# Expert groups of one mixture layer: 68 groups of two batches become 60 whole groups and eight half groups in float32, and their results go through DRAM instead of into sums by batch

## The reference, cut to what matters

```python
rw = softmax(router_logits); w, sel = top_k(rw, 2)          # per batch
def mlp(x, g, u, d):  return (gelu(x @ g) * (x @ u)) @ d     # 256 -> 1024 -> 256
out = sum over the two chosen experts e:  w[e] * mlp(x, gate[e], up[e], down[e])
out = out + mlp(x, shared_gate, shared_up, shared_down)
x = x + out                                                  # then layers 1, 2 and 3
```

## Time and profile before

| | |
|---|---|
| time, median of 3 runs | 1223.13 us (1220.38 to 1224.0) |
| the profiled execution | 1221.87 us, its span 1220.3 us |
| PE busy | 1195.6 us, 98% of the span |
| DVE / ACT / POOL busy | 719.9 / 466.1 / 469.6 us |
| chain that ended last | PE 91%, DVE 4%, the rest under 2% each |
| DMA | 135.31 MB, mean 111 GB/s |

### The profile page before, as it was taken

How to read it: one execution, slowest core, us unless ns; L and a number is a source line. 1 busy time by engine, 2 the same in 40 slices (tenths; PEclk the granted TensorE clock), 3 DMA queues, 4 the chain that set the end, 5 groups by cost and what they waited for, 6 DMA issues and landing times.

```text
span 1220.3 us, 26642 instructions
## 1 busy us (share of the span) xinstructions
PE 1195.6 (98%) x7370; PEld 1043.2 (85%) x7371; DVE 719.9 (59%) x1282; ACT 466.1 (38%) x877; POOL 469.6 (38%) x297
## 2 busy tenths in 40 slices
PE   8898999999999999999999999999999999899998
PEld 7798998888888888888888888889999998778876
DVE  5789686556557557566565656555555556444443
ACT  4256532322222222223223223233443333466664
POOL 2076689406336036081444563010000002875840
PEclk9899999999999999999999999999999999999999
DMA  7159772202213013021131321033344336476654
GB/s 221 44 189 312 258 265 83 83 15 65 66 32 99 15 32 99 15 86 45 47 86 45 86 67 30 17 109 103 106 110 107 98 87 236 144 238 214 205 154 121
DMA packets 133169, 135.31 MB, mean 111 GB/s; under 512 B 64640, under 2 KB 114048, under 8 KB 131072
## 3 DMA queue, kind: packets, MB, share of 16 engines
q1 hardware_dynamic: 119440, 84.87, 23.3%
q0 software_dynamic: 13680, 49.81, 13.1%
HBM read 109.48 MB, written 25.17 MB: 110 GB/s over the span
## 4 chain that ended last, share of the span: by engine, by line
PE 91%; DVE 4%; POOL 1%; issue 1%; ACT 1%; DMA 1%; SPq 0%; DVEq 0%; ACTq 0%; POOLq 0%
PE bank L630 15%; PE bank L632 15%; PE bank L631 15%; PE bank L686 10%; PE bank L1015 6%; PE bank L667 5%; PE bank L685 4%; PE bank L1044 3%; PE bank L858 2%; PE bank L737 2%; PE bank L993 2%; PE bank L739 2%; PE bank L738 2%; PE bank L688 1%; PE bank L1024 1%
## 5 line engine op out<-in xcount | busy, mean ns | idle before, releaser
L474 POOL TENSOR_TENSOR W<-raw,one 128x1024 fp32r<-128x1024 f32 x79 | 150.3, 1902 | 577.3 <-PE bank L686 349.5
L1631 DVE TENSOR_TENSOR FS<-bank,FS 128x512 f32<-128x512 f32 x200 | 138.1, 691 | 193.1 <-PE bank L632 162.8
L1102 ACT ACTIVATE FS<-bank 128x512 f32<-128x512 f32 x200 | 119.5, 597 | 322.8 <-PE bank L632 322.5
L630 PE MATMUL bank<-W,RS 128*128 (+1 forms) x576 | 225.7, 392 | 2.3 <-DVE W L1726 2.0
L632 PE MATMUL bank<-W,RS 128*128 (+1 forms) x576 | 224.9, 390 | 0.0
L631 PE MATMUL bank<-W,RS 128*128 (+1 forms) x576 | 224.8, 390 | 0.0
L686 PE MATMUL bank<-W,RS 128*128 x544 | 216.2, 419 | 0.0
L476 POOL TENSOR_TENSOR W<-raw,W 128x1024 fp32r<-128x1024 f32 x79 | 191.8, 2428 | 6.2
L1699 DVE SCALAR_TENSOR_TENSOR acc<-bank,weight,acc 64x256 f32 x272 | 131.4, 483 | 73.7 <-issue 36.9
L1109 ACT ACTIVATE RS<-bank 128x512 fp32r<-128x512 f32 x144 | 86.4, 600 | 176.2 <-PE bank L667 176.2
L630 PE MATMUL bank<-RS,W 128*128 128x256 f32 x448 | 129.9, 290 | 0.0
(11 more groups left out here) (221 smaller groups left out, 2075.2 us busy)
## 6 DMA issues: line engine op xcount, KB each, us to landing
raw<-in_w POOLq DMA_DIRECT2D x87, 512.0 KB, 4.2
mixes<-acc SPq DMA_DIRECT2D x16, 1024.0 KB, 5.6
W<-mixes SPq DMA_DIRECT2D x16, 1024.0 KB, 6.2
FS<-in_xT SPq DMA_DIRECT2D x200, 64.0 KB, 2.5
acc<-in_w SPq DMA_DIRECT2D x22, 512.0 KB, 4.2
acc<-in_b SPq DMA_DIRECT2D x8, 640.0 KB, 11.0
acc<-in_x SPq DMA_DIRECT2D x32, 128.0 KB, 3.8
raw<-in_mask POOLq DMA_DIRECT2D x8, 512.0 KB, 4.6
```

What stands on the lines that cost most here:

```text
L474: pool.tensor_tensor(hi, raw[:, k, :], ones_like(PIECE), ALU.mult).then_inc(done, 1)
L630: pe.matmul(ps, ah, bh, start=(i == 0), stop=False)
L1102: act.activation(gl[h], gate_ps[h][:, :], ACT.Gelu_apprx_tanh).then_inc(gelu_done, 1)
L1631: TT(hid[h], up_ps[h][:, :], gl[h], ALU.mult).then_inc(hid_done, 1)
```

## The change: what it does

1. Chosen groups. There are again 68 positions, but 60 of them are whole groups (128 tokens, one expert, `floor(count / 2)` for each expert) and four times two are half groups: the up to eight batches that are left over go in twos, whatever their experts, through half of the hidden units in one position (`HALVES`, positions 4 and 12 of a loop body of 16) and through the other half in another. Half groups multiply in plain float32 (`up_gate_mixed`, `down_mixed`), with weights that SP loads unsplit into `acc` rows (`load_mixed0`, six pieces for each half group).
2. Results. A whole group's result is added up in SBUF by two instructions (L1879, L1883 of the changed kernel), and `store_chosen` writes it to `chosen_rows` in DRAM by slot. In the late stage `load_chosen` brings the eight halves (64 x 256) for each unit back by eight DMAs, and `join` adds them; `cross_over` on ACT is gone, as is POOL's clearing of `acc` (`zeros_made`).
3. Routing. The tables have other contents, and their computation is cut into more and shorter portions: some after groups 2 and 3, then portions in pairs 0 to 4. `tables_ready` is now incremented in the fifth pair (index 4), and the sums on PE (`route_sums_`) stand within pair 0.
4. POOL frees a weight slot by `add_step` in place of `down_done`, and begins with layer 3's first expert after the last join (`x1_done`, NU) in place of shortly before the last down products.
5. In the last units DVE does `x2_lo` before `keep`.

The core of the diff:

```diff
-NR0 = (2 * NB + E) // 2
+NMIXED0 = E // 2
+FULL0 = NB - NMIXED0
+NR0 = FULL0 + 2 * NMIXED0
+HALVES = (4, 12)
@@ PE
+            def both_batches(ps, stationary, weights_of, n, start, stop):
+                for j in range(2):
+                    half = slice(S * j, S * (j + 1))
+                    mm = pe.matmul(ps[half, 0:n], stationary[:, half], weights_of[j], start=start, stop=stop,
+                                   skip_group_check=True)
+                return mm
+            def up_gate_mixed(g, at, h):
...
+                for ps, k, done in ((gate_ps[h], 0, gate_done), (up_ps[h], 1, up_done)):
...
+                    for c in range(DC):
+                        part = slice(c * 512 + D * h, c * 512 + D * (h + 1))
+                        mm = both_batches(ps, chunk(xm, c), [mixed0_w[2 * k + j][:, part] for j in range(2)], D,
+                                          c == 0, c == DC - 1)
@@ PE, pair 0
                     up_gate_shared(g, xset, q)
+                    if first and q == 3:
+                        route_sums_()
@@ PE, chosen groups
-            with pe.Fori(S0 // 2 + 1, S1 // 2) as pair:
-                group(2 * pair, 0)
-                group(2 * pair + 1, 1)
+            with pe.Fori(0, NMIXED0) as m:
+                for k in range(BODY):
+                    chosen_group(S0 + 2 + BODY * m + k, k % 2, place_at(m, k), place_at(m, k - 1))
@@ SP
+            def store_chosen(g, r, at):
+                sp.wait_ge(acc_done, g + 1)
...
+            def load_chosen(n, u, buffer, after=None):
...
+                for i in range(4):
+                    for w in range(2):
+                        sp.dma_start(chosen_in[buffer][w][S * (i % 2):S * (i % 2) + S, i // 2, :],
...
@@ DVE
-                for part_, done_ in ((0, add_step), (1, acc_done)):
...
+                    TS(scaled, out_ps[p][:, D:2 * D], weight, None, ALU.mult).then_inc(add_step, 1)
...
+                STT(chosen_out[p], out_ps[p][:, 0:D], weight, scaled if at.half is None else held, ALU.mult, ALU.add)\
+                    .then_inc(acc_done, 1)
@@ DVE, routing
-                elif (pair, q) == (2, 3):
-                    route_dests()
...
+                elif (pair, q) == (4, 1):
+                    route_group_turns(1, turn3)
+                elif (pair, q) == (4, 2):
+                    route_sources()
@@ DVE, late units
-                keep(n + 1)
-                x2_lo(n + 1)
-                if not last:
+                    x2_lo(n + 1)
+                    keep(n + 1)
+                else:
+                    keep(n + 1)
+                    x2_lo(n + 1)
+                    join(n + 2, k + 1, 1)
```

More of the change, by code:

```diff
@@ L26 @@
+from collections import namedtuple
 from contextlib import ExitStack
@@ L1444, in route_weights @@
+                done(op)
                 done(TT(rc, w1c, w2c, ALU.add))
                 done(dve.reciprocal(rc, rc))
-                for w in (w1c, w2c):
-                    done(TT(w, w, rc, ALU.mult))
-                    done(TS(col(28), w, TOP_SCALE, None, ALU.mult))
-                    done(STT(w, w, 1.0 - TOP_SCALE, col(28), ALU.mult, ALU.add))
-            groups, sum1, sum2, ends, begins, places = (blocks(k) for k in (104, 120, 136, 152, 168, 184))
-            present, turns = blocks(248), blocks(264)
@@ L1478, in route_places @@
-            def route_places():
-                ints = small[:, 88:104].bitcast(I32)
-                TS(ints[:, 0:E], counts[:, 16:24], 1.0, None, ALU.add)
-                done(TS(ints[:, E:2 * E], counts[:, 24:32], 0.0, None, ALU.add))
+                for t, m, w, _ in pairs:
+                    op = TS(w, w, rc, None, ALU.mult)
+                done(op)
+                for t, m, w, part in pairs:
+                    op = TS(part, w, TOP_SCALE, None, ALU.mult)
+                done(op)
@@ L1484, in route_places, with route_groups @@
+                for t, m, w, part in pairs:
+                    op = STT(w, w, 1.0 - TOP_SCALE, part, ALU.mult, ALU.add)
+                done(op)
+            def route_groups():
+                ints = spare.rearrange("b a e -> b (a e)").bitcast(I32)
+                done(TS(ints, counts[:, 16:32], 0.0, None, ALU.add))
                 done(TS(ints, ints, 1, None, ALU.logical_shift_right))
@@ new lines, in route_places @@
+            def route_places():
+                done(STT(places, begins, 2.0, ranks_, ALU.mult, ALU.add))
+                TT(left, left, places, ALU.subtract)
+                done(STT(spare, groups, 2.0, ranks_, ALU.mult, ALU.is_le))
+                done(TT(left, left, spare, ALU.mult))
+                done(TT(places, places, left, ALU.add))
+                terms_ = ((spare[:, 0, :], M1, 0, pos1), (spare[:, 1, :], M2, 0, pos2), (junk, M1, 1, pos3))
+                for t, m, a, _ in terms_:
+                    op = TT(t, places[:, a, :], m, ALU.mult)
+                done(op)
+                for t, _, _, pos in terms_:
+                    op = dve.tensor_reduce(pos, t, AX.X, ALU.add)
+                done(op)
@@ L1703, in group @@
-            def group(g, p, n=3, after=1, add_before=add, skipped=TURNLESS, xset=1, after_shared=False):
+                f = at.full if at.half is None else FULL0 + at.mixed
+                weight = weight0[:, bass.ds(f, 1)]
+                if at.half == 0:
+                    TS(held, out_ps[p][:, 0:D], weight, None, ALU.mult).then_inc(acc_done, 1)
+                    return
+                if at.half is None:
+                    TS(scaled, out_ps[p][:, D:2 * D], weight, None, ALU.mult).then_inc(add_step, 1)
+                    dve.wait_ge(add_step, at.full + 1)
```

554 lines of the change are left out of this document (339 added, 215 removed).

## The result

The changed kernel takes **1243.04 us** (median of 4 runs, 1240.77 to 1245.42); the kernel before, on the same chip, 1222.46. The ratio is 1.017, with an interval of 1.0144 to 1.0195: about 21 us slower. The forecast was 1207 (1193 to 1218), so it had the wrong sign and missed by 36 us.

What follows compares the result with a forecast made beforehand. PE was taken to bound the kernel, working 1195.6 of 1220.3 us. The terms -23.7 - 0.9 + 1.5 + 10.7 + 2.5 - 6.3 sum to -16.2 us, giving a median of 1207 us, range 1193 to 1218 for 8 in 10.

Steps and rivals of the forecast that it cites:

- The longer loop bodies I cost at nothing: Chosen groups: longer loop bodies add no time, as PE's straight code and late-stage jumps show no pause.
- The fallback that the prediction named: Chosen-group loop: if a jump back did cost 1 us, it would be 3 to 4 us in all.
- jumps back: Loop over chosen groups: PE's jumps back in the longer bodies were costed at nothing.
- half groups: Chosen groups: eight whole groups become half groups of 6.2 us, 3.0 less each, -23.7 us in all.
- The end of my own bounds: Chosen groups: a half group takes 7.0 us with a 0.8 us wait in each for ACT and DVE, -17 in all.
- start and pairs: After group 3 and pair 0, -0.9 us (-6 to +4); pairs 1 to 4, +1.5 us (-3 to +5).
- the disturbed case: Pair 0: one or two DVE waits beside POOL at each of two places, plus half a clock dip: 5.5 us (0.5 to 10).
- the first chosen expert: Group S0: later tables_ready delays POOL's fifth piece, so PE waits 10.7 us mid-group.
- the clock: Behind the wait in group S0: PE's slower clock adds 2.5 us.
- joins: Late stage: eight DMAs per join cost nothing, as SP has some 9.5 us of work in each 14.6 us unit.
- the end of the late stage: Last join and x2_lo: POOL waiting and x2_lo going first gain 6.3 us (2 to 9).
- DVE late in the pairs: Rival, pairs: eight DVE portions lose 1.5 us each on PE, +10 us more, 1217 us; chance 0.12.

Runs made afterwards that it cites:

- e1: Changed kernel with the loop over the four long bodies written out on PE, ACT, DVE and SP: 1220.83 us, ratio 0.9968 to the kernel before.
- e4: Kernel before the change, with its loop body lengthened from two groups to 16 on PE, ACT and DVE: 1232.98 us, ratio 1.0067.
- e3: Changed kernel, all loops kept, with each body's first half group's weight loads issued at its third and fourth group: 1233.48 us.
- e13: e4 plus four unused 512 KB transfers issued by SP with the inputs of each body's third group: 1240.25 us, ratio 1.0124.
- e14: Changed kernel with loop written out, places and slots portions earlier, first expert's loads early; half of the half groups' products left out: 1186.04 us.
- e7: e1 with POOL's first stacking work held back until DVE has finished the slots portion of pair 0: 1221.98 us, ratio 0.9975.
- e5: e1 with POOL starting the first chosen expert on an earlier semaphore, chosen_ready, in place of tables_ready: 1219.46 us, ratio 0.9953.
- e2: Changed kernel with the loop over the long bodies written out on PE alone: 1221.15 us, ratio 0.997 to the kernel before.

## Why the prediction was wrong, point by point

**The step that failed** is "The longer loop bodies I cost at nothing". It rested on straight code and on jumps in the late stage, whose bodies are short (472 instructions of PE in the program, 432 of them products and transposes; the chosen loop has 1,339 and 728, and had 183 and 96 before; weight loads not counted), and on no row of a long body that jumps. The fallback that the prediction named, 1 us for a jump, was eight times too small, and it was never made a rival. It cost 24.2 us of span. Of these 17.3 are standing, and PE's busy time for the same instructions is 5.9 us longer than in e1 (1184.5 against 1178.6), which fits the lower clock behind the pauses. The two halves of it, length and collision, are shown by e4, e3 and e13.

The Trainium skill's page "Runtime: NRT & Kernel Launch", section "Instruction fetch mechanics", has the mechanism, and the prediction did not use it: a taken branch whose target is no longer among the instructions that an engine holds makes it fetch them by DMA, over a queue of its own, before it can go on. The runs agree where they can: the wait ends on nothing that the profile shows, a body of 16 groups has it and one of two has not, q8 makes 42 transfers more with the long body (e4), the wait goes when the loop is written out, and it grows from 1.8 to 5.1 us at the first jump with other transfers on the DMA engines (e4, e13: 1.45 + 0.33 and 1.45 + 3.62). That section of the Trainium skill lets TensorE hold 2,048 instructions. As each product has a weight load beside it (7406 and 7407 in the rows of the profile after), an estimate by it is 1,339 + 728 = 2,067 instructions for the long body, hardly more than are held, and 472 + 432 = 904 for the longest that jumped without a pause. No run here tells where between these the pause begins, and the skill gives no price.

**The ledger**, spans, forecast 1204.1 against 1243.8 (39.7 apart):
- jumps back: 0 forecast, +24.2.
- half groups: -23.7 forecast, -17.6; the size was off by 6.1, the mechanism right (e14). The end of my own bounds (7.0 us for each) was right for the wrong reason, since nobody waits.
- start and pairs: by PE's arrival at the second half of S0 (184.68 in the earlier trace rows; 200.78 less the wait of 10.10 is 190.68), +6.0 where +0.6 was forecast. The wait at `route_sums_` was one of 8.3 us and not one or two of some 2; in pairs 1 to 4 PE waits 8.2 us in 8 places (3.4 in 3 before). I had the disturbed case in the text and priced it by one row, where five were hit.
- the first chosen expert: 10.7 forecast, 10.1; the clock 2.5, and 2.1. The difference held though both of its sides moved: `tables_ready` came at 166.0 us and not at 160.5, and PE 6.0 us late as well, both behind the same delayed stages. That both move with PE stands in the prediction.
- joins: 0, and no `turn_x1` waited for a DMA: right.
- the end of the late stage: -6.3 forecast. The rows that answer to the earlier trace rows are, for PE and DVE:

```profile
1062.51 0.60 PE L983 MATMUL bank<-ident,routing 128*128 128x128 f32 x4
...
1070.43 0.45 PE L711 MATMUL bank<-W 128*128 128x384 f32 x1 [1.84 <-DVE W L2004]
```

```profile
1070.30 2.65 DVE L1997 TENSOR_TENSOR raw<-routing 128x512 f32<-128x512 f32 x1
```

The first wait is gone, but the second is 1.84 us as before: `x2_lo` waited there for ACT, and its order on DVE was not what held it. From the last chosen transposes (833.02; 806.41 before) to layer 3's first product (1075.49; 1052.95 before) 4.1 us are gained, and from there to the end 1.0 is lost.
- Together these leave 1.8 us. Most of it is in the jumps: in the changed kernel's own timeline they take 25.8 us, and e1, against which they are 24.2, comes to its first chosen transposes 1.0 us later (206.57 against 205.60). With 25.8 the remainder is 0.2.

**The rivals.** "DVE late in the pairs" had its mechanism right and was given 0.12; it was no rival but a part of what happened. The rule behind it, from the Trainium skill's page "SBUF — State Buffer", section "Who interferes with whom", is borne out: in pair 0 of the changed kernel L1666, L1673 and L1679 took 2.3 to 2.5 us; in e7 they fell to 0.3 us with POOL quiet; a tensor_reduce that lay wholly inside one instruction of POOL (L1738 at 143.98 us, POOL's from 143.82 to 146.33) took 0.63 us and was not held to its end; and e5 made the same loss anew. The five held rows of pair 0 took 10.2 us longer than in e7, which is the wait of 8.3 us and the slack that DVE had.

The range failed with the sign: none of its cases held a cost of jumps.

## What to carry to other kernels

A loop body that grows from a few groups to sixteen has to be priced at its jump back as a cost of its own, and transfers that start at the head of a body fall on just that moment: issue them some groups later, or write the loop out where PE is the bound. When a wait is taken away by letting an engine start earlier, ask beside which instructions of its neighbour it now runs; twice here a wait of 8 to 10 us came back elsewhere, by POOL beside DVE in one case and by a held POOL ahead of ACT in the other. Give a disturbed stretch the price of all its instructions that can be hit, and not that of the one row that shows it.

## What the runs showed of the hardware that was not expected

- A jump back of PE in a body of 16 groups costs 1.8 us of standing by itself, 4.6 with 2 MB of DMA issued at it (e4, e13); in the changed kernel 2.4 and 5.8 (e3, after). Bodies of 96 and of 432 products and transposes (the chosen loop before, the late stage) showed no pause; the long body of the changed kernel has 728. Where between these it begins was not tried.
- The pause has two parts some instructions apart. The first is 1.4 to 2.0 us with and without the loads; only the second grows, from 0.5 to 0.9 us (e3) to 3.7 to 4.5 us in the changed kernel.
- The jumps of ACT, DVE and SP, which have slack here, cost PE nothing (e2). On PE the jump can also cost the clock: 0.50 from 364 to 370 us after 5.9 us of standing, and 0.83 from 360 to 370 after 2.0 us in e3. In e4 it stayed at 1.00 after 1.8 us at the first jump and read 0.83 from 496 to 506 us after 2.0 us at the second.
- PE's instruction queue moved 28 transfers in the kernel before and 70 in e4, for the same products: the 33 passes through a body of two groups were not fetched anew, the four through a body of 16 were.
